# Reordering ACT's and DVE's work at the last attention step and at the change to the feed-forward, and other operations in the gating

## The reference

```
x = x + attention(x)        # 32 query heads, 8 key heads, 512 cached and 128 new keys per sequence
x = x + x W1.T + 0.5 (x A1[label]) B1.T
x = x + x W2.T + 2 sum over e of gates[e] (x A2[e]) B2[e]   # 8 experts, the two best by x Wr + 5 onehot(lang)
x = x + down(silu(gate(x)) * up(x))      # 512 -> 1376 -> 512, each of the three with a LoRA chosen by sequence
```

## Time and profile before

| | |
|---|---|
| median of 3 runs | 1431.28 us (1429.61 to 1434.79) |
| span of the profiled execution | 1428.2 us; its time outside the span is not listed |
| PE busy | 1392.2 us, 97% of the span |
| DVE busy | 1107.4 us, 78% |
| ACT busy | 844.1 us, 59% |
| POOL busy | 807.6 us, 57% |
| the chain that ended last, by engine | PE 88%, DVE 7%, ACT 2%, issue 1% |

### The profile page before, as it was taken

How to read it: one execution, slowest core, us unless ns; L and a number is a source line. 1 busy time by engine, 2 the same in 40 slices (tenths; PEclk the granted TensorE clock), 3 DMA queues, 4 the chain that set the end, 5 groups by cost and what they waited for, 6 DMA issues and landing times.

```text
span 1428.2 us, 26905 instructions
## 1 busy us (share of the span) xinstructions
PE 1392.2 (97%) x8004; PEld 1206.9 (85%) x8004; DVE 1107.4 (78%) x2243; ACT 844.1 (59%) x2076; POOL 807.6 (57%) x801
## 2 busy tenths in 40 slices
PE   5999999999999999999999999999999998899999
PEld 4788888888888888888888888888888787788887
DVE  7888888888888888888888888888888566545543
ACT  4666666666666676676666666666676322333332
POOL 6555555555555666666666666665566320444442
PEclk9999999999999999999999999999999999999999
DMA  6333333433333232222222322222423430343341
GB/s 237 91 106 111 100 102 105 114 105 101 101 102 107 69 81 66 69 65 66 66 65 66 79 68 66 65 65 48 122 52 106 109 91 23 92 130 115 121 122 67
DMA packets 191553, 129.87 MB, mean 91 GB/s; under 512 B 118833, under 2 KB 158513, under 8 KB 188977
## 3 DMA queue, kind: packets, MB, share of 16 engines
q1 hardware_dynamic: 190448, 126.84, 32.5%
q0 software_dynamic: 384, 1.05, 0.2%
q10 hardware_dynamic: 576, 0.27, 0.1%
HBM read 125.25 MB, written 24.64 MB: 105 GB/s over the span
## 4 chain that ended last, share of the span: by engine, by line
PE 88%; DVE 7%; ACT 2%; issue 1%; POOL 0%; DVEq 0%
PE banks L322 20%; PE banks L323 20%; PE banks L324 20%; PE banks L1364 11%; PE banks L1338 10%; PE banks L1302 2%; DVE pt_pair L936 1%; DVE prob L961 1%; ACT prob L727 1%; ACT pt_pair L723 1%; PE banks L1579 1%; PE banks L1593 1%; PE banks L1406 1%; PE banks L1310 1%; PE banks L1532 1%
## 5 line engine op out<-in xcount | busy, mean ns | idle before, releaser
L727 ACT ACTIVATE prob<-prob,nbias 128x640 f32<-128x640 f32 x256 | 210.2, 822 | 153.2 <-DVE nbias L961 153.2
L936 DVE TENSOR_TENSOR pt_pair<-banks,pt_pair 128x640 fp32r<-128x640 f32 x256 | 210.8, 823 | 107.0 <-ACT pt_pair L723 104.6
L961 DVE CUSTOM_DVE_ANT_0 prob<-banks,mask,q_rs 128x640 f32<-128x640 f32 x256 | 220.0, 878 | 38.0 <-PE banks L324 38.0
L1364 PE MATMUL banks<-w_pair,o_pair 128*128 128x512 f32 x768 | 224.1, 414 | 0.3 <-DVE o_pair L936 0.3
L723 ACT ACTIVATE pt_pair<-banks 128x640 fp32r<-128x640 f32 x256 | 179.3, 700 | 48.3 <-PE banks L1338 48.3
L1338 PE MATMUL banks<-ident,prob 128*128 128x128 f32 x1280 | 185.0, 275 | 4.7 <-DVE pt_pair L936 4.1
L1338 PEld LDWEIGHTS banks<-ident,prob 128*128 128x128 f32 x1280 | 146.4, 140 | 49.0 <-issue 37.8
L322 PE MATMUL banks<-w_pair,x_pair 128*128 128x256 f32 (+1 forms) x512 | 178.9, 349 | 7.9 <-DVE w_pair L1014 7.9
L323 PE MATMUL banks<-w_pair,x_pair 128*128 128x256 f32 (+1 forms) x512 | 173.5, 339 | 0.0
L324 PE MATMUL banks<-w_pair,x_pair 128*128 128x256 f32 (+1 forms) x512 | 172.8, 337 | 0.0
L322 PE MATMUL banks<-kt_pair,qt_pair 128*128 128x320 f32 x512 | 164.3, 321 | 1.4 <-DVE qt_pair L936 1.4
(11 more groups left out here) (188 smaller groups left out, 3436.9 us busy)
## 6 DMA issues: line engine op xcount, KB each, us to landing
w_raw<-in_w_att SPq DMA_DIRECT2D x56, 320.0 KB, 3.2
w_raw<-in_fw SPq DMA_DIRECT2D x66, 256.0 KB, 3.5
x_raw<-in_xT SPq DMA_DIRECT2D x64, 256.0 KB, 3.3
kt_all<-in_kT SPq DMA_DIRECT2D x128, 128.0 KB, 2.5
kv_raw<-in_kv SPq DMA_DIRECT2D x384, 32.0 KB, 1.7
kt_raw<-kt_all SPq DMA_DIRECT2D x38, 256.0 KB, 3.0
kv_raw<-in_kv SPq DMA_DIRECT2D x608, 16.0 KB, 1.6
fb_all<-in_gu_b SPq DMA_DIRECT2D x32, 176.0 KB
```

Source lines behind the costliest of these rows:

```text
L727: act.activation(prob[:, h, :], prob[:, h, :], ACT.Exp, bias=nbias[:, h:h + 1], scale=-1.0, accum_out=psum_row[:, h:h + 1]).then_inc(exped, 1)
L936: dve.tensor_tensor(pair[1], src, pair[0].bitcast(F32), ALU.subtract).then_inc(lo_sem, 1)
L961: dve.tensor_tensor_reduce(out=prob[:, h, :].rearrange("p (a n) -> p a n", a=2), in0=score_ps[h % 2][:, :, 0:HALF], in1=mask[:, n % B, :]. ...
L1364: last = pe.matmul(misc_ps, o_pair[:, j, h, :], w_pair[:, k, ds(at + h * HID, HID)], start=i == 0, stop=i == 3 * REP - 1)
```

## The change

It edits four lists and leaves TensorE's and SP's as they are.

- **Last attention step.** ACT does `pt_high(n - 1, 3)` ahead of the exponents of heads 0 and 1, and `low_high(0)` ahead of `pt_high(n, 0)`. DVE does `pt_low(n - 1, 3)` right after `mask_min` of head 0, `x1t_low(0)` ahead of `normalise(n, 1)`, and `lora1_low(0)` ahead of `pt_low(n, 0)`.
- **Gating.** The two `tensor_scalar` become a `tensor_tensor` and a `scalar_tensor_tensor` that read the per-row value as a broadcast operand.
- **First tiles of the feed-forward.** ACT does `gu_high(0, 0)` before stage 5 instead of 6, and POOL waits with `gu_low(0, 0)` until the gating of sequence 5 is over. After `exponent_gate(7)` ACT takes a Sigmoid of one column of `spare`, and `gu_high(1, 1)` comes before `gate_up_lora_high(1)`, with a wait for the last `block1_lora`. Then follow the sigmoid of tile 0, `dn_high(0, 0)`, `x3t_high(7)` and `act_high(0, 0)`. DVE does `fb_low(0, 0)` ahead of `gate_up_lora(0)`, the low half of `gate_up_lora(1)` after `hgt_low(7)`, and after `end_b(7)` first `gsig` of tile 0, then `fb_low(1, 1)`, `x3t_low(7)` and the rest of `gated(0, 0)`.
- **`d_b`.** Its rounding and its low part go from the change to the feed-forward to tile 6 on both engines.

The diff, cut to its core:

```diff
 # POOL
+            pool.wait_ge(gates, GSTEPS * (B - 2))
             gu_low(0, 0)
...
 # ACT
             def final_step(n, par):
+                pt_high(n - 1, 3)
                 exponent(n, par, 0)
                 exponent(n, par, 1)
-                pt_high(n - 1, 3)
                 x1t_high(0)
                 v_high(n, par)
                 exponent(n, par, 2)
                 o_high(n - 1)
+                low_high(0)
                 pt_high(n, 0)
-                low_high(0)
...
             for b in range(1, B - 1):
-                if b == B - 2:
+                if b == B - 3:
                     gu_high(0, 0)
                 stage(b)
             gate_up_lora_high(0)
             exponent_gate(B - 1)
+            act.activation(spare[:, 0:1], spare[:, 2:3], ACT.Sigmoid)
             x3t_high(B - 2)
+            act.wait_ge(y1_done, B)
+            gu_high(1, 1)
             gate_up_lora_high(1)
             hgt_high(B - 1)
-            x3t_high(B - 1)
-            act.wait_ge(s_ffs, 16 * 5 * B)
-            act.activation(db_pair[:, 0], d_b[:], ACT.Copy).then_inc(db_hi, 1)
+            def down_b_high():
+                act.wait_ge(s_ffs, 16 * 5 * B)
+                act.activation(db_pair[:, 0], d_b[:], ACT.Copy).then_inc(db_hi, 1)
...
             def ff_step(m, par):
-                gu_high(m, par)
-                dn_high(m - 1, 1 - par)
-                swish(m - 1, 1 - par)
+                if m == 1:
+                    sigmoid(0)
+                    dn_high(0, 0)
+                    x3t_high(B - 1)
+                    act_high(0, 0)
+                else:
+                    gu_high(m, par)
+                    dn_high(m - 1, 1 - par)
+                    swish(m - 1, 1 - par)
...
 # DVE
-                dve.tensor_scalar(logits[:], logits[:], top[:], None, ALU.subtract).then_inc(gates, 1)
+                dve.tensor_tensor(logits[:], logits[:], top[:].broadcast_to([P, E]), ALU.subtract).then_inc(gates, 1)
...
-                dve.tensor_scalar(gate[:], gate[:], grec[:], LORA2_SCALE, ALU.mult, ALU.mult).then_inc(gates, 1)
+                dve.scalar_tensor_tensor(out=gate[:], in0=gate[:], scalar=LORA2_SCALE, in1=grec[:].broadcast_to([P, E]),
+                                         op0=ALU.mult, op1=ALU.mult).then_inc(gates, 1)
...
             def final_step(n, par):
                 mask_min(n, par, 0)
+                pt_low(n - 1, 3)
                 mask_min(n, par, 1)
                 normalise(n, 0)
-                pt_low(n - 1, 3)
+                x1t_low(0)
                 normalise(n, 1)
-                x1t_low(0)
                 mask_min(n, par, 2)
...
                 o_low(n - 1)
+                lora1_low(0)
                 pt_low(n, 0)
-                lora1_low(0)
...
+            fb_low(0, 0)
             gate_up_lora(0)
             gating(B - 1)
             x3t_low(B - 2)
-            gate_up_lora(1, u_ps, (tg_lo, 1))
+            gate_up_lora_own(1, u_ps, (tg_lo, 1))
             hgt_low(B - 1)
+            gate_up_lora_low(1)
...
-            fb_low(0, 0)
             end_b(B - 1)
+            gate_sigmoid(0)
+            fb_low(1, 1)
             x3t_low(B - 1)
-            low(db_hi, 1, [db_pair[:, k] for k in range(2)], d_b[:], db_lo)
+            gated(0, 0)
             def ff_step(m, par):
-                fb_low(m, par)
-                gated(m - 1, 1 - par)
+                if m > 1:
+                    fb_low(m, par)
+                    gated(m - 1, 1 - par)
```

More of the change, by code:

```diff
@@ L888, in dn_high, with sigmoid, act_high, swish @@
                 act.activation(fw_pair[par][:, F_DOWN:FW], fw_raw[par][:, F_DOWN:FW], ACT.Copy).then_inc(dn_hi, 1)
-            def swish(m, par):
+            def sigmoid(m):
                 act.wait_ge(g_done, m + 1)
                 act.activation(sig[:], g_ps, ACT.Sigmoid).then_inc(sig_done, 1)
+            def act_high(m, par):
                 to_high(act_pair[par][:, 0], act_f[:], act_done, m + 1, act_hi)
+            def swish(m, par):
+                sigmoid(m)
+                act_high(m, par)
             def ff_step(m, par):
-                gu_high(m, par)
-                dn_high(m - 1, 1 - par)
-                swish(m - 1, 1 - par)
-            tiles(ff_step, (2, lambda: gate_up_lora_high(2)), (3, lambda: gate_up_lora_high(3)),
+                if m == 1:
[7 more added lines that the diff above has]
+                    swish(m - 1, 1 - par)
+            tiles(ff_step, (2, lambda: gate_up_lora_high(2)), (3, lambda: gate_up_lora_high(3)), (6, down_b_high),
                   (FT + 1, lambda: down_lora_high(0)))
@@ L1196, in stage, with gate_up_lora_own @@
                     x1t_low(b + 2)
-            def gate_up_lora(n, bank=tg_ps, used=None):
+            def gate_up_lora_own(n, bank=tg_ps, used=None):
                 dve.wait_ge(tg_done, n + 1)
@@ L1206, in gate_up_lora, with gate_up_lora_low @@
                                   ALU.mult).then_inc(tg_own, 1)
+            def gate_up_lora_low(n):
                 dve.wait_ge(tg_hi, n + 1)
@@ L1211, in gate_up_lora @@
                                   ALU.subtract).then_inc(tg_lo, 1)
[L1213 to L1218, removed]
-            gate_up_lora(1, u_ps, (tg_lo, 1))
-            hgt_low(B - 1)
+            def gate_up_lora(n, bank=tg_ps, used=None):
+                gate_up_lora_own(n, bank, used)
+                gate_up_lora_low(n)
             def fb_low(m, par):
@@ L1226, in fb_low, with gate_sigmoid, gated @@
                                   ALU.subtract).then_inc(fb_lo, 1)
-            def gated(m, par):
+            final_step(NT - 1, 1)
+            for b in range(1, B - 1):
+                stage(b)
+            fb_low(0, 0)
+            gate_up_lora(0)
+            gating(B - 1)
+            x3t_low(B - 2)
+            gate_up_lora_own(1, u_ps, (tg_lo, 1))
+            hgt_low(B - 1)
+            gate_up_lora_low(1)
+            def gate_sigmoid(m):
                 dve.wait_ge(sig_done, m + 1)
                 dve.tensor_tensor(gsig[:], g_ps, sig[:], ALU.mult).then_inc(gsig_done, 1)
+            def gated(m, par):
+                if m:
+                    gate_sigmoid(m)
                 dve.wait_ge(gsig_done, m + 1)
@@ L1249, in add_ffn, with down_b_low @@
                     dve.tensor_tensor(acc[:, b, :], ffn_bank[b % HB], acc[:, b, :], ALU.add).then_inc(ffn_added, 1)
-            fb_low(0, 0)
+            def down_b_low():
+                low(db_hi, 1, [db_pair[:, k] for k in range(2)], d_b[:], db_lo)
             end_b(B - 1)
+            gate_sigmoid(0)
+            fb_low(1, 1)
             x3t_low(B - 1)
-            low(db_hi, 1, [db_pair[:, k] for k in range(2)], d_b[:], db_lo)
+            gated(0, 0)
             def ff_step(m, par):
-                fb_low(m, par)
-                gated(m - 1, 1 - par)
+                if m > 1:
+                    fb_low(m, par)
+                    gated(m - 1, 1 - par)
             tiles(ff_step, (2, lambda: gate_up_lora(2, used=(tg_lo, 2))), (3, lambda: gate_up_lora(3, used=(tg_lo, 3))),
+                  (6, down_b_low),
                   (FT + 1, lambda: (down_lora(0, (tg_lo, 4)), add_ffn(0))))
```

## The result

The changed kernel took 1421.78 us (median of 4 runs, 1417.91 to 1422.59) against 1430.79 us for the kernel before (1429.61 to 1434.79, 4 runs): a ratio of 0.9923, with a 95% interval of 0.9907 to 0.9938. The profiled execution took 1422.34 us, of which 1.84 us lie outside its span.

What follows compares the result with a forecast made beforehand. TensorE, whose program is unedited, was taken as the bound, so only its idle or low-clock time could return: 8.95 + 1.6 + 0.4 = 10.95 us off 1431.28 gives 1420.3 us, range 1416.8 to 1424.5.

Steps and rivals of the forecast that it cites:

- The change to the feed-forward: Before `gate_up(1)`: the 6.45 us idle and the low clock's 2.50 us both go, 8.95 us in sum.
- the third rival: Before `gate_up(1)`: the stall becomes a wait for tile 1's low weights; about 1428.8 us, chance 0.06.
- The table load: On ACT ahead of 1204.21: 1.28 us in idle time, costing nothing; with a drain, total 1421.7 us.
- Gating: Stage 6: moving POOL's piece returns TensorE's 1.52 us wait and 0.1 more, 1.6 us; bounds 1.5 and 1.8.
- The last step: Last attention step: `block1(0)` starts at 1108.5 instead of 1108.86, 0.4 us gained; ends -0.3 and 1.7.
- The rest of the step follows TensorE: Last attention step: after `block1(0)` everything simply follows TensorE; no further gain or loss priced.
- the rival on the slower side: Before `block1(0)`: one 2.5 us idle piece drops the clock to 0.50; 40 us of it gives 1440, chance 0.04.

Runs made afterwards that it cites:

- e5: Changed kernel with `gu_high(1,1)` put behind `x3t_high(7)` on ACT; 1428.24 us (one run).
- e7: Changed kernel without the Sigmoid of one column, so its table is loaded at the gate's own sigmoid; 1422.15 us (one run).
- e4: Changed kernel with the new gating forms, but `gu_high(0,0)` and POOL's piece where they were before; 1422.16 us (one run).
- e8: Changed kernel with the old gating forms, but POOL's piece where the change put it; 1417.85 us (one run).
- the second profile of before: The kernel before, run again unedited; 1431.38 us (one run), tail 330.96.
- the three sets: The changed kernel measured three times unedited against the kernel before: 1421.78, 1421.2 and 1421.3 us.
- e6: Changed kernel with `normalise(n,1)` ahead of `x1t_low(0)` and three unused DVE reductions ahead of `o_low`; 1421.74 us (one run).
- the third profile of the changed kernel: The changed kernel unedited, a third time; 1421.3 us (six runs), tail 320.53.

## Why the prediction was right, and where it was not

The forecast of 1420.3 us (1416.8 to 1424.5) is 1.5 us below the median measured first and 0.9 to 1.0 below the other two. Step by step:

- **The change to the feed-forward: 8.95 forecast.** Both parts came: no wait is left, and the clock is 1.00. Against the execution that the forecast was made from it is 12.31 - 3.22 = 9.09 us; against the other one 7.98, since there the stretch at 0.50 cost 1.1 less. The idle time, 6.45, is the same in all three profiles that have it; the clock's part is not. The margins were as told: `gsig` ends 1.85 us ahead of `gate_up(1)` (2.0 forecast), `act_f(0)` 0.9 us ahead of the up half (1.0). `hgt_low(7)`, whose cover the forecast called thin (1207.1 against 1207.17), had 1.89 us to spare: it ended at 1206.79, and its product started at 1208.68. e5 shows that the weights would have been next to be late, as the third rival has it, and near its price: 1428.24 (one run) against 1428.8.
- **The table load: nothing forecast.** Right: it took 1.28 at 1202.34, and the Sigmoid behind it started at 1203.63. The drain that the Trainium skill counts ("ScalarE: Activation LUTs", What ACT_TABLE_LOAD costs) shows in no row here, ahead of the load or behind it, nor in e7. That the load also holds POOL's piece back was not in the forecast.
- **Gating: 1.6 forecast,** 1.79 measured, the upper bound (1.8). That the forms shield nothing was argued from the held `fb_low` and the Trainium skill's rule on two SBUF inputs ("SBUF — State Buffer", Who interferes with whom). e4, e7 and e8 agree: 2.33 and 2.37 us for new forms beside POOL, 0.23 for the old ones clear of it.
- **The last step: 0.4 forecast; this step failed in part.** Its chain was right in detail: `v_low` led by 0.12 us, `normalise(1)` was held for 1.79, and `block1(0)` came 0.51 earlier. What failed is "The rest of the step follows TensorE": behind the idle piece, which had become a single one of 2.47 us, the clock fell, and from `block1(0)` to the transposes of `p(n,1)` it took 4.90 instead of 14.51 - 11.19 = 3.32, so 1.58 were lost and the step ended 1.07 us behind. The forecast had this as the rival on the slower side. Its place and its sign were right and its size far off: one stretch of some 3 us instead of up to 40. Its argument against it, the clock of 1.00 in the earlier trace rows, was one execution of a thing that varies: against the second profile of before, with its own fall, the step gains 16.06 - 15.57 = 0.49, near the 0.4 forecast, because the fall of the clock cost about the same, 1.6 us, in each of the two.
- **The sum.** 1417.3 was forecast for the span. To 1420.5 it is 3.2: 2.2 for the later mark (the scatter of the first 62 us, not the change), 1.47 for the last step (-0.4 forecast, +1.07 measured), less 0.19 in the gating and 0.14 at the change to the feed-forward, less 0.1 elsewhere. Adding the 3.1 us by which the median lay above the span hid 1.3 us of this: 1.84 us lie outside the span after, and 1431.38 - 1429.6 = 1.78 outside that of the second profile of before, so, by estimate, the profiled execution of before, 1428.2 long, was some 1.3 us shorter than the median. The total gain, 10.95, is to be held against 9.0, 10.8 and 11.1 us between the medians of the three sets, and 9.9 to 10.4 us between the tails. That the time came out so near is in part luck: the last step went the other way, and the gating, the change to the feed-forward and the difference between span and median made up for some of it.

What makes the clock fall behind one idle piece and not behind an equal one stays open, and so does why the first 62 us scatter.

## What to carry to other kernels

Idle time on TensorE is worth more than its length where the clock falls behind it, and whether it falls can differ from one execution to the next: before a term of the sum leans on "the clock stayed at 1.00" or on the length of a stretch at 0.50, it wants a second profile. The `tensor_scalar` of `normalise(1)` and the operations with two inputs in SBUF, the memory that holds the tiles (e4, e7), were held to about the end of POOL's piece when POOL led by 0.05 to 0.12 us. Not every operation is: after, `hgt_low(7)`, which reads one of its tiles from PSUM (`banks` in the rows, where TensorE's results stand), took 0.29 us as before, beside POOL's piece of 1205.35 to 1207.75; the operation behind it, with both inputs in SBUF, took 1.47 instead of 0.68. So look for the order of starts on the two timelines, and move the piece rather than change the form. An operation that costs nothing where it stands may still set when another engine starts: ask that before it is dropped.

## What was not expected of the hardware

- The clock fell behind idle pieces of 2.06 to 2.68 us in some executions only. Of the nine profiles with 2.41 to 2.68 us before `block1(0)` it fell in eight (e8 is the ninth); of the three with 2.06 or 2.07 us before the values in two; of the two with 0.87 and 0.89 us in none, nor behind the 1.09 or 1.10 us before `block1(0)` in the three with the order of before, nor behind the 1.45 to 1.52 us in stage 6 of four profiles.
- When it fell differed as well: after, the products behind the idle piece start some 0.23 apart until 1112.06, 1.5 us on, and in e6 until 1110.78, 0.84 us on, while in e5 and in the third profile of the changed kernel the first product already takes 0.59 to the next start and the next five 0.42 or 0.43 each.
- The gate half behind one and the same idle piece of 6.45 us took about 5.25, 4.28 and 4.15 us up to its LoRA product in three executions.
- Two instructions 0.05 to 0.12 us apart on two engines decided about 1.2 to 2.2 us of DVE's time.
